# Five of eight token lists ahead of an attention loop, three inside it, both heads of a pair in one product

## The reference

```python
routing_scores = jax.nn.sigmoid(routing_logits)
attn = jnp.einsum('bhqd,bhkd->bhqk', q, k) / jnp.sqrt(jnp.float32(D))
k_keep = max(1, int(tgt_len * SPARSITY))            # int(2048 * 0.4) = 819
_, top_idx = jax.lax.top_k(rs_t, k_keep)
keep = keep.at[..., top_idx].set(True)
sparse = jnp.where(keep[:, :, None, :], attn, NEG_INF)
w = jax.nn.softmax(sparse.astype(jnp.float32), axis=-1).astype(q.dtype)
out = jnp.einsum('bhqk,bhkd->bhqd', w, v)
```

## Time and profile before

| | |
|---|---|
| median of 3 runs (547.59, 550.35, 551.19) | 550.35 us |
| the profiled execution: its time, its span | 547.99 us, 546.0 us |
| mean granted clock of PE | 0.852 |
| PE busy | 446.5 us (82%) |
| DVE busy | 390.0 us (71%) |
| ACT busy | 310.2 us (57%) |
| POOL busy | 207.7 us (38%) |

### The profile page before, as it was taken

One profiled execution on the slowest core, in us unless ns is written; L12 is line 12 of the kernel. 1 busy time (PEld: TensorE's weight loads), 2 busy tenths in 40 slices (PEclk: granted clock), 3 DMA queues, 4 the chain that ended last, 5 costly groups with the idle time before them and its releaser, 6 DMA issues.

```text
span 546.0 us, 9548 instructions
## 1 busy us (share of the span) xinstructions
PE 446.5 (82%) x3286; PEld 224.0 (41%) x3286; DVE 390.0 (71%) x1042; ACT 310.2 (57%) x447; POOL 207.7 (38%) x282
## 2 busy tenths in 40 slices
PE   3775587689999999999999999999999670039993
PEld 3341576222434333343343433434333260039992
DVE  8788832785888898888888887898889443014661
ACT  3436000025777787777877777778778630036661
POOL 3200477602340534534434444351003004604886
PEclk9888555555999999998999998999999955559998
DMA  7733300035010010010010010010000010141331
GB/s 229 116 115 116 98 8 8 3 121 192 4 33 2 6 33 4 6 35 4 5 33 3 6 35 3 4 33 3 2 2 2 28 52 25 53 116 12 26 33 7
DMA packets 26346, 22.04 MB, mean 40 GB/s; under 512 B 6272, under 2 KB 22464, under 8 KB 26304
## 3 DMA queue, kind: packets, MB, share of 16 engines
q1 hardware_dynamic: 15632, 16.56, 10.0%
q0 software_dynamic: 7296, 2.96, 4.7%
q10 hardware_dynamic: 3376, 1.98, 2.0%
HBM read 12.89 MB, written 8.93 MB: 40 GB/s over the span
## 4 chain that ended last, share of the span: by engine, by line
PE 63%; DVE 16%; POOL 7%; issue 6%; DMA 3%; ACT 3%; POOLq 1%; SPq 0%; DVEq 0%; ACTq 0%
PE OP L1402 17%; PE ST L1386 12%; PE ST L1366 6%; PE SC L1344 6%; DVE tile_max L1001 6%; POOL out L633 5%; PE SC L1342 4%; PE SC L1297 4%; PE OP L1410 2%; POOL slots_dram L625 2%; DVE PR L867 2%; DMA QS<-MT 2%; DMA KV<-slots_dram 1%; PE OP L1483 1%; PE SC L1513 1%
## 5 line engine op out<-in xcount | busy, mean ns | idle before, releaser
L1001 DVE TENSOR_REDUCE tile_max<-SC 128x1 f32<-128x410 f32 (+1 forms) x512 | 271.1, 576 | 45.1 <-PE SC L1342 41.8
L726 ACT ACTIVATE PR<-ST 128x1024 f32<-128x1024 f32 (+1 forms) x224 | 208.2, 961 | 50.0 <-PE ST L1386 49.2
L539 POOL DMA_INDIRECT G<-kv_dram,idx x104 | 109.4, 1052 | 163.3 <-ACT PR L726 102.7
L1386 PE MATMUL ST<-QS,KT 51*128 51x512 bf16 (+1 forms) x416 | 107.5, 394 | 2.7 <-DMA QS<-MT 2.3
L1402 PE MATMUL OP<-PR,VS 128*32 128x512 f32 x768 | 106.6, 628 | 0.4 <-ACT PR L726 0.4
L1342 PE MATMUL SC<-KT,QS 48*128 48x410 bf16 x256 | 78.6, 363 | 1.8 <-ACT KT L692 1.0
L1386 PEld LDWEIGHTS ST<-QS,KT 51*128 51x128 bf16 (+1 forms) x416 | 29.1, 96 | 50.9 <-issue 36.6
L1344 PE MATMUL SC<-KT,QS 48*128 48x409 bf16 x128 | 46.5, 363 | 3.6 <-DVE tile_max L1001 0.3
L633 POOL DMA_INDIRECT out<-PR,owner x24 | 37.6, 1568 | 28.5 <-issue 27.5
L1346 PE MATMUL SC<-KT,QS 48*128 48x358 bf16 x128 | 42.7, 333 | 0.0
L1366 PE MATMUL ST<-C,OS 128*128 128x32 f32 x248 | 38.8, 281 | 0.2
(11 more groups left out here) (240 smaller groups left out, 535.8 us busy)
## 6 DMA issues: line engine op xcount, KB each, us to landing
kv_dram<-KV SPq DMA_DIRECT2D x4, 512.0 KB, 2.9
WE<-in_w_fc SPq DMA_DIRECT2D x1, 2048.0 KB, 10.2
WE<-in_w_proj SPq DMA_DIRECT2D x1, 2048.0 KB, 15.1
G<-kv_dram,idx POOLq DMA_INDIRECT x104, 2.4
slots_dram<-zeros ACTq DMA_DIRECT2D x1, 1548.0 KB, 11.1
KV<-slots_dram SPq DMA_DIRECT2D x1, 1548.0 KB, 7.5
q_parts_dram<-QP SPq DMA_DIRECT2D x3, 512.0 KB, 3.8
QS<-q_parts_dram SPq DMA_DIRECT2D x16, 96.0 KB
```

The costliest lines, as they stand in the source:

```text
L539: pool.indirect_dma_start(G[:, i % 2, slot_of(s), :], None, kv_dram, bass.IndirectOffsetOnAxis(ap=idx[:, i, s:s + 1].bitcast(U32), axis=0) ...
L726: nc.scalar.activation(PR[:, k, 0:cols], ST[:, (KSTEPS * n + k) % 2, 0:cols], ACT.Exp, scale=float(D) ** -0.5).then_inc(exp_done, 1)
L1001: v.tensor_reduce(tile_max[:, n % 2, at_col:at_col + 1], bank(RING_AT["unit", u])[:, 0:410 - f], AX.X, ALU.max).then_inc(s_reduced, 1)
L1386: last = mm(ST[:, at_step % 2, 512 * e:512 * e + 512], KT[rows, i % 2, P * tile:P * tile + P], QS[rows, i % 2, CHUNK * c:CHUNK * (c + 1)], ...
```

## The change

`index_mm` takes both heads of a pair in one product: the stationary side has 28 columns (14 for each head), the moving side 128 (64 for each head), 16 products for a pair where there were 32. `A1` keeps its layout. The result holds both heads' blocks (and two cross blocks that nothing uses); ACT copies it in one activation `[28 x 128]` where there were two of `[14 x 64]`, and `row_to_partition` takes four products, accumulated by twos, where there were two.

The lists of pairs 0 to 4 (`AHEAD = 5`) are made in front. Behind them `columns` makes the `B1` of pairs 5 to 7, and then come the keys of pair 0. The lists of pairs 5, 6 and 7 are made in chunks 2, 6 and 10: the one-hot on DVE after 5 of the chunk's 16 maxima, the product on PE behind step 2, the copy on ACT behind the copy of the turned output, the turn on PE behind step 4, and `index` on DVE after the eleventh maximum. PE waits for `idx` before it weighs, since the turned list lies in `OP`. The memset of `by_code` goes.

```diff
+AHEAD = 5
+LIST_BESIDE = {NQ * (i - AHEAD) + 2: i for i in range(AHEAD, NP)}
...
         def tokens_of(i):
 
-            return SC[:, [0, 2][i % 2], 0:HALF], [OP[:, 0:STEPS], ST[:, 0, 0:STEPS]][i % 2]
+            if i >= AHEAD:
+                return OP[0:2 * CODES, 0:P], OP[:, P:P + STEPS]
+            return SC[0:2 * CODES, [0, 2][i % 2], 0:P], [OP[:, 0:STEPS], ST[:, 0, 0:STEPS]][i % 2]
...
-            sp.wait_ge(idx_ready, NP)
+            sp.wait_ge(columns_ready, 4)
...
-            for i in range(NP):
+            def copy_codes(i):
                 act.wait_ge(idx_mm, i + 1)
                 if i >= 2:
                     act.wait_ge(row_mm, i - 1)
-                for e in range(2):
-                    rows = slice(32 * e, 32 * e + CODES)
-                    nc.scalar.activation(by_code[rows, i % 2, :], tokens_of(i)[0][rows, :], ACT.Copy)\
-                        .then_inc(code_copied, 1)
+                nc.scalar.activation(by_code[:, i % 2, :], tokens_of(i)[0], ACT.Copy).then_inc(code_copied, 1)
+
+            for i in range(AHEAD):
+                copy_codes(i)
...
                     copy_ot(n - 1)
+                if n in LIST_BESIDE:
+                    copy_codes(LIST_BESIDE[n])
                 weights(n, 4, 3)
...
-            columns(0, 2, 1)
+            columns(0, 1, 1)
             onehot(0)
-            columns(2, 4, 2)
+            columns(1, 2, 2)
             onehot(1)
             index(0)
-            columns(4, H, 3)
-            for i in range(2, NP):
+            columns(2, AHEAD, 3)
+            for i in range(2, AHEAD):
                 onehot(i)
                 index(i - 1)
-            index(NP - 1)
+            index(AHEAD - 1)
+            columns(AHEAD, NP, 4)
...
-                units(min(first, NU), min(first + 10, NU))
+                units(min(first, NU), min(first + 5, NU))
+                if n in LIST_BESIDE:
+                    onehot(LIST_BESIDE[n])
+                units(min(first + 5, NU), min(first + 10, NU))
                 if n % NQ == 1 and n >= NQ:
                     reciprocal(n // NQ - 1)
-                units(min(first + 10, NU), min(first + UPC, NU))
+                units(min(first + 10, NU), min(first + 11, NU))
+                if n in LIST_BESIDE:
+                    index(LIST_BESIDE[n])
+                units(min(first + 11, NU), min(first + UPC, NU))
...
-                for e in range(2):
-                    for t in range(NT):
-                        last = mm(tokens_of(i)[0][32 * e:32 * e + CODES, :], B1[:, 2 * i + e, t, :], A1[:, i % 2, e, :, t],
-                                  start=(t == 0), stop=(t == NT - 1), skip_group_check=True)
+                for t in range(NT):
+                    last = mm(tokens_of(i)[0], B1[:, i, t, :, :].rearrange("p e c -> p (e c)"), A1[:, i % 2, :, :, t],
+                              start=(t == 0), stop=(t == NT - 1), skip_group_check=True)
                 last.then_inc(idx_mm, 1)
...
                 for hi in range(2):
-                    last = mm(tokens_of(i)[1][HALF * hi:HALF * (hi + 1), :], by_code[:, i % 2, :], to_row[0:64, hi, :],
-                              start=True, stop=True)
+                    for e in range(2):
+                        last = mm(tokens_of(i)[1][HALF * hi:HALF * (hi + 1), :], by_code[:, i % 2, HALF * e:HALF * (e + 1)],
+                                  to_row[0:2 * CODES, e, hi, :], start=(e == 0), stop=(e == 1))
...
-                    pe.wait_ge(idx_ready, NP)
+                    pe.wait_ge(idx_ready, AHEAD)
...
                         turn_k(n // NQ + 1)
+                    if k == 2 and n in LIST_BESIDE:
+                        pe.wait_ge(o_copied, n)
+                        index_mm(LIST_BESIDE[n])
                     if k == 4:
+                        if n in LIST_BESIDE:
+                            row_to_partition(LIST_BESIDE[n])
+                            pe.wait_ge(idx_ready, LIST_BESIDE[n] + 1)
                         weigh(n, (0, 1), first=True)
```

More of the change, by code:

```diff
@@ L112, in constants @@
     cols["code"] = np.broadcast_to(np.arange(CODES), (P, CODES))
[L113 removed]
+    to_row = np.zeros((P, 2, 2, STEPS))
     for e in range(2):
         for c in range(CODES):
[L116 removed]
+            to_row[CODES * e + c, e, c % 2, 6 * e + c // 2] = 1
     cols["to_row"] = to_row.reshape(P, -1)
@@ L211, in build @@
         lo_of = sb("lo_of", [P, H, NT], FP16)
-        key_of = sb("key_of", [P, H, NT], FP16)
+        key_of = sb("key_of", [P, NP, NT, 2], FP16)
         place16 = sb("place16", [P, HALF, NT], FP16)
@@ L216, in build @@
         B0 = WE.rearrange("p n c -> p (n c)")[:, 0:H * NT * CODES // 2].bitcast(FP16)\
-            .rearrange("p (h t c) -> p h t c", h=H, t=NT)
-        by_code = sb("by_code", [64, 2, HALF])
-        B1 = sb("B1", [P, H, NT, CODES], FP16)
+            .rearrange("p (i t e c) -> p i t e c", i=NP, t=NT, e=2)
+        by_code = sb("by_code", [2 * CODES, 2, 2 * HALF])
+        B1 = sb("B1", [P, NP, NT, 2, CODES], FP16)
         idx = sb("idx", [P, NP, STEPS], I32)
@@ L446, in _ @@
             sp.wait_ge(qparts_out, 16 * PARTS)
-            sp.wait_ge(qs_zero, 3)
+            sp.wait_ge(qs_zero, 2)
             def load_q(i):
@@ L795, in _ @@
             dve.wait_ge(dve_step, next_step())
-            v.memset(by_code[:, :, :], 0.0).then_inc(qs_zero, 1)
             for r in (32, 96):
@@ L922, in _, with columns @@
                 .then_inc(places_ready, 1)
-            v.tensor_copy(key_of[:, :, :].rearrange("p h t -> p t h"), key_int[:, :].rearrange("p (t h) -> p t h", h=H))\
+            v.tensor_copy(key_of[:, :, :, :].rearrange("p i t e -> p t i e"),
+                          key_int[:, :].rearrange("p (t i e) -> p t i e", i=NP, e=2))\
                 .then_inc(places_ready, 1)
-            def columns(h0, h1, step):
-                n = h1 - h0
-                v.tensor_tensor(B0[:, h0:h1, :, :], key_of[:, h0:h1, :].rearrange("p h (t a) -> p h t a", a=1)
-                                .to_broadcast([P, n, NT, CODES]),
-                                cc("code").rearrange("p (h t c) -> p h t c", h=1, t=1).to_broadcast([P, n, NT, CODES]),
+            def columns(i0, i1, step):
+                n = i1 - i0
+                shape, by_tile = [P, n * NT * 2, CODES], "p i t e c -> p i t (e c)"
+                v.tensor_tensor(B0[:, i0:i1].rearrange("p i t e c -> p (i t e) c"),
+                                key_of[:, i0:i1, :, :].rearrange("p i t (e a) -> p (i t e) a", a=1).to_broadcast(shape),
+                                cc("code").rearrange("p (h c) -> p h c", h=1).to_broadcast(shape),
                                 ALU.is_equal).then_inc(column_step, 1)
                 dve.wait_ge(column_step, step)
-                v.tensor_tensor(B1[:, h0:h1, :, :], B0[:, h0:h1, :, :],
-                                token.rearrange("p (h t c) -> p h t c", h=1, c=1).to_broadcast([P, n, NT, CODES]),
+                v.tensor_tensor(B1[:, i0:i1].rearrange(by_tile), B0[:, i0:i1].rearrange(by_tile),
+                                token.rearrange("p (h t c) -> p h t c", h=1, c=1).to_broadcast([P, n, NT, 2 * CODES]),
                                 ALU.mult).then_inc(columns_ready, 1)
```

11 lines of the change are left out of this document (4 added, 7 removed).

## The result

| | before | after |
|---|---|---|
| median, the two timed side by side | 548.97 us | 572.69 us (570.19 to 573.94, 4 runs) |
| ratio, 95% interval | | 1.0424 [1.0366, 1.0481] |
| profiled execution: time, span | 547.99, 546.0 us | 570.19, 568.3 us |
| mean granted clock of PE | 0.852 | 0.836 |

What follows compares the result with a forecast made beforehand. PE was taken to bound the loop, with DVE and ACT near full. Front -10.2, three lists +13.5 and clock dips +2.6 gave +5.9 us on a median of 550.35: 556 us, range 546 to 563.

Steps and rivals of the forecast that it cites:

- The front: Lists of pairs 0 to 4 ahead of the loop: pair 0's keys start at 83.6 instead of 94.01, gaining 10.2 us.
- (a): List chunks, between steps 2 and 3: PE waits for DVE's one-hots and starts the list product 1.65 us late.
- (b): List chunks: the 16 merged products at the full clock take 0.115 us each, half of 0.23, together 1.85 us.
- the first rival: List product in the loop: strided reading takes a fixed time at any clock, 3.7 us; about 562 us, chance 0.20.
- 0.23 in the loop: Sign of being wrong: merged list products 0.23 us apart in the loop, where 0.115 was forecast.
- (c): Step 4 of list chunks: copy, turn and `idx` let PE weigh at 187.85 instead of 186.62, 1.25 us later.
- (d): Step 3 of list chunks: PE's wait of 0.25 us for DVE goes, since DVE has caught up.
- The clock: List chunks: PE's granted clock dips to 0.50 in two of three, 1.3 us each, 2.6 us in all.
- the price by product: Front and loop: a merged product costs what a small one does, 0.115 us at low clock; 546 us, chance 0.20.
- the shorter waits: Loop: DVE runs ahead, so PE's wait for the one-hots goes; 551 us, chance 0.12 shared with in-between product prices.
- no dips: List chunks: PE keeps its clock, the other terms hold; 553.7 us, chance 0.14 for one dip or none.

## Why the prediction was wrong in size

- **The front**: right, 10.4 us against 10.2, and its terms too (0.23 us for a merged product against 0.23; a pair 4.77 against 4.85; keys from 83.77 against 83.6). The prediction let the price go with the columns; the distances show that it goes with the 16-byte lines they touch, which is the same at 32 bytes apart. So the rule of the Trainium skill that spoke against the merge held.
- **(a) the wait for the one-hots**, 1.65: 1.76. Right.
- **(b) the product**, "so I halve 0.23 as well: 0.115 each, 1.85 us": this step failed. It was 3.81, the same time at either clock, 2 us a list. The error was to take the ratio from the transposes, which read neighbours, for a product that the same rows had shown to be held by its reading. This was the first rival, which was right in its mechanism and gave 562, and "0.23 in the loop" was one of the prediction's own signs of being wrong.
- **(c) the wait in step 4**, 1.25: 0.98 from turn to weighing. Right enough. **(d)** isn't visible beside the rest.
- **The clock**, "a dip costs 1.3 us", "a dip in two of three": this step failed most. All three chunks dipped, for 10.2, 13.65 and 13.65 us instead of the 3.4 of the earlier trace rows, and in chunk 6 that is 4.5 us. Over three lists the loop lost 31.2; forecast were 13.5 + 2.6 = 16.1. Of the 15.1 missing, some 6 are the product (3 x 2) and the other 9 the clock. The dip of the earlier trace rows came in a chunk whose longest wait of PE ahead of it was 0.37 us; it was no measure of one with 6.5 us of waiting and slow reading.
- **The rivals**: the price by product (546) and the shorter waits (551) are refuted by the rows above; "no dips" as well.
- **The direction** came out for the reason given: more is lost in the loop than gained in front.

What brings the long stretches is only shown in pieces. A wait of PE can, without slow reading: with columns side by side the clock fell inside the wait of 2.8 us in two of three chunks and stayed low for 17 us, and at 16 bytes, in one execution, a wait of 2.02 us in chunk 1 had 13.65 us behind it. Slow reading can, without a wait: 3.4 us where it stands in step 4 beside other work, and 6.8 to 10.2 in the old place with both waits filled (in an execution 3.7 us above its median). With neither the wait of 1.76 us nor the slow product there were still 6.8 us in two of three chunks, begun as the turn stood ahead of the weighing. With everything moved beside other work, at 4 bytes, there was none in the list chunks. The parts don't add up to the whole, and the same kernel had 3.4 us in one execution and 10 to 14 in another. What sets the length stays open. Only argued is why the old place is worse: the narrow products of step 3 (the transposes of the maxima and of the output) follow the list product directly there, and the second wait follows these.

## What to carry to other kernels

Before matmul work is merged or moved, look at how far apart its moving columns lie: once every column is in another 16-byte line, fewer and wider products save nothing, and a faster clock doesn't either. Here the merge by itself changed nothing that the intervals can tell (ratio 1.003), the move by itself lost 4.8%, and the merge with a layout of 4 bytes apart, at no cost to the one-hots, gained 2.2%. Where PE is full, work that is added must bring neither a wait nor a slow reader, and its price is the instruction plus the wait plus what a lower clock does to all that stands behind: 10 us here for 3.8 us of products, and 2.2 us once placed beside other work with both gone.
